# Stores and loads of y: single pairs on ScalarE's queue in place of batches on SyncE's

## What is computed

```python
def dynamic_depthwise(x, w1, b1, w2, b2):      # layers 0, 2 and 3
    pooled = x.mean(axis=(2, 3))
    hdn = relu(pooled @ w1 + b1)
    kernels = (hdn @ w2 + b2).reshape(b, 32, 3, 3)   # one 3x3 kernel per sample and channel
    return depthwise_conv(x, kernels, pad=1)

def sign_conv(x, W):                           # layer 1
    return conv(sign(x), sign(W), pad=1)       # 32 channels to 32
```

## Time and profile before

| | |
|---|---|
| median of 3 runs | 4350.15 us (4338.25 to 4359.49) |
| the profiled execution, its own time | 4354.15 us |
| its span, first to last instruction | 4352.3 us |
| granted TensorE clock, mean | 0.873 of full speed |
| busy, TensorE matmuls | 3142.5 us (72%) |
| busy, VectorE | 2069.2 us (48%) |
| busy, ScalarE | 1786.4 us (41%) |
| busy, GpSimd | 1957.0 us (45%) |
| moved by DMA | 829.46 MB, mean 191 GB/s |
| queue q1 (SyncE) | 734.28 MB, 66.5% of 16 engines' span |
| queue q10 (ScalarE) | 76.68 MB, 8.2% |
| issue to landing, median | load of a batch 26.1 us, store 23.6 us, early channel 6.4 us |

### The profile page before, as it was taken

One profiled execution on the slowest core, in us unless ns is written; L12 is line 12 of the kernel. 1 busy time (PEld: TensorE's weight loads), 2 busy tenths in 40 slices (PEclk: granted clock), 3 DMA queues, 4 the chain that ended last, 5 costly groups with the idle time before them and its releaser, 6 DMA issues.

```text
span 4352.3 us, 69714 instructions
## 1 busy us (share of the span) xinstructions
PE 3142.5 (72%) x26176; PEld 2008.6 (46%) x26176; DVE 2069.2 (48%) x6038; ACT 1786.4 (41%) x2626; POOL 1957.0 (45%) x3175
## 2 busy tenths in 40 slices
PE   0675987758876588865887667867778759777598
PEld 0443645435454354633545434554445535445355
DVE  2626643266432764327543275333844257432573
ACT  2433633335333463434534354333543436324232
POOL 1326544264432653336533464425643265431754
PEclk9987998879988798987998879888889889888799
DMA  6288697876969769596694967969678697786946
GB/s 210 57 147 168 151 318 200 155 164 140 340 175 170 159 159 322 159 195 153 182 330 119 212 148 197 306 118 216 149 217 292 109 212 165 234 270 111 200 76 218
DMA packets 589270, 829.46 MB, mean 191 GB/s; under 512 B 489731, under 2 KB 490502, under 8 KB 572550
## 3 DMA queue, kind: packets, MB, share of 16 engines
q1 hardware_dynamic: 323200, 734.28, 66.5%
q10 hardware_dynamic: 216582, 76.68, 8.2%
q0 software_dynamic: 49152, 14.05, 2.0%
HBM read 375.89 MB, written 267.45 MB: 148 GB/s over the span
## 4 chain that ended last, share of the span: by engine, by line
PE 46%; DMA 21%; DVE 9%; SPq 8%; ACT 5%; POOL 4%; ACTq 3%; issue 3%; DVEq 0%; POOLq 0%
PE acc L961 26%; PE acc L978 14%; SPq L327 6%; DMA dense_out<-arena 5%; DMA out<-y 4%; DMA arena<-x 4%; POOL y L510 4%; PE acc L1040 3%; DMA arena<-signs 3%; DVE dense_stats L860 2%; DMA signs<-arena 2%; DMA arena<-y 2%; ACT arena L599 2%; ACTq L535 2%; ACTq L606 2%
## 5 line engine op out<-in xcount | busy, mean ns | idle before, releaser
L961 PE MATMUL acc<-y,arena 64*128 64x384 f32 x9216 | 1749.3, 508 | 190.1 <-ACT y L568 129.0
L961 PEld LDWEIGHTS acc<-y,arena 64*128 64x128 f32 x9216 | 1013.6, 197 | 777.4 <-ACT y L568 229.2
L327 POOL DMA_DIRECT2D arena<-y x1536 | 790.6, 522 | 837.3 <-PE acc L978 736.4
L568 ACT ACTIVATE y<-acc 128x768 f32<-128x768 f32 x832 | 645.1, 807 | 1177.5 <-PE acc L978 1176.6
L978 PE MATMUL acc<-arena 64*128 64x384 f32 x4608 | 953.9, 509 | 195.2 <-issue 195.2
L489 POOL TENSOR_SCALAR arena<-arena,cst,fill 128x24 f32<-128x24 f32 (+1 forms) x1536 | 614.3, 419 | 701.8 <-issue 450.4
L510 POOL TENSOR_TENSOR y<-arena,y 128x3072 f32<-128x3072 f16 x88 | 529.8, 6043 | 734.5 <-DMA arena<-dense_out 734.3
L860 DVE BATCH_NORM_STATS2 dense_stats<-y 128x6 f32<-128x192 f32 x1536 | 408.0, 345 | 728.4 <-POOL y L510 728.2
L978 PEld LDWEIGHTS acc<-arena 64*128 64x128 f32 x4608 | 518.1, 196 | 422.3 <-issue 228.2
L1040 PE MATMUL acc<-arena,wd_side 128*32 128x384 fp8e4 (+1 forms) x10752 | 470.4, 329 | 290.3 <-DMA arena<-signs 231.5
L802 DVE TENSOR_SCALAR_CACHE_REDUCE y<-acc 128x768 f32<-128x768 f32 x256 | 245.1, 958 | 624.3 <-PE acc L978 624.3
(11 more groups left out here) (84 smaller groups left out, 1145.6 us busy)
## 6 DMA issues: line engine op xcount, KB each, us to landing
y<-x SPq DMA_DIRECT2D x64, 2304.0 KB, 26.1
out<-y SPq DMA_DIRECT2D x64, 2304.0 KB, 23.6
arena<-y SPq DMA_DIRECT2D x768, 141.0 KB
arena<-x SPq DMA_DIRECT2D x168, 576.0 KB, 6.4
dense_out<-arena ACTq DMA_DIRECT2D x384, 192.0 KB, 6.9
arena<-dense_out SPq DMA_DIRECT2D x192, 384.0 KB, 6.8
arena<-y SPq DMA_DIRECT2D x768, 71.9 KB
arena<-signs SPq DMA_DIRECT2D x192, 250.0 KB, 10.4
```

The lines of the kernel that those rows point to most:

```text
L327: eng.dma_start(halo[at:at + n, slot, :, d0:d0 + size], y[source:source + (n - 1) * step + 1:step, first + odd:first + odd + 3:2, s0:s0 + ...
L568: nc.scalar.activation(y[:, 2 * g:2 * g + 2, k * KN:(k + 1) * KN], acc[:, 2 * k:2 * k + 2, 0:KN], ACT.Identity, accum_out=sums[:, g, k:k + ...
L961: nc.tensor.matmul(acc[:, 2 * k + odd, 0:KN], w_center[at, slot, 2 * q + odd, :], y[at, 2 * g + odd, k * KN:(k + 1) * KN], start=turn == 0 ...
```

## The change

Every pair of channels becomes a transfer of its own (1152 KB), with its own semaphores `loaded[g]` and `stored[g]`. ScalarE issues the store of pair g of layer 3 right behind its evictions of that pair, and then, from g = 5 on, waits for the store of pair g - 5 and issues the next sample's load of it. The last five loads (pairs 11 to 15) are issued in pairs 0 to 4 of the next layer 0, behind ScalarE's eviction and ahead of `pair_signs`. SyncE keeps the first loads of sample 0, halos, early channels and sign writes. VectorE in place of ScalarE reads the eight early channels (24 to 31) of layer 3, one in each of pairs 0 to 7, behind its eviction. Waits follow: GpSimd's clearing of the stage and SyncE's loads of early channels wait for VectorE's count too, the halos of layer 0 and TensorE for single pairs.

```diff
+LOAD_LAG = 5
...
     if li == 0:
-        return [c for c in range(C) if c % BATCH_CH < 2] if s == 0 else list(range(AHEAD_FIRST, C))
+        return [c for c in range(C) if c % BATCH_CH < 2] if s == 0 else list(range(AHEAD_FIRST, AHEAD_FIRST + PAIRS))
...
 def dve_channels(s, li):
-    return [c for c in range(C) if c not in act_channels(s, li)]
+    rest = [c for c in range(C) if c not in act_channels(s, li)]
+    return rest[AHEAD_FIRST:] + rest[:AHEAD_FIRST] if li == 0 and s > 0 else rest
...
+        def load(eng, s, g):
+            at = slice(2 * g, 2 * g + 2)
+            eng.dma_start(y[:, at, :].rearrange("p c n -> p (c n)"),
+                          x[s, :, at].rearrange("p c g w -> p (c g w)")).then_inc(loaded[g], 16)
+
+        def store(eng, s, g):
+
+            wait_evicted(eng, (s * ND + ND - 1) * PAIRS + g + 1)
+            at = slice(2 * g, 2 * g + 2)
+            eng.dma_start(out[s, :, at].rearrange("p c g w -> p (c g w)"),
+                          y[:, at, :].rearrange("p c n -> p (c n)")).then_inc(stored[g], 16)
+
+        def load_next(eng, s, g):
+
+            eng.wait_ge(stored[g], 16 * (s + 1))
+            load(eng, s + 1, g)
...
             if li == 0:
-                eng.wait_ge(loaded[b], 16 * (s + 1))
+                for g in range(b * BATCH_PAIRS, (b + 1) * BATCH_PAIRS):
+                    eng.wait_ge(loaded[g], 16 * (s + 1))
...
-                    if i >= AHEAD_SLOTS:
-                        sp.wait_ge(act_stat, stat_count(act_channels, s, 0) + i - AHEAD_SLOTS + 1)
+                    last = i - AHEAD_SLOTS
+                    if last >= PAIRS:
+                        sp.wait_ge(dve_stat, stat_count(dve_channels, s, ND - 1) + last - PAIRS + 1)
+                    elif last >= 0:
+                        sp.wait_ge(act_stat, stat_count(act_channels, s, 0) + last + 1)
...
-                    store(s, b)
-                    if s < B - 1:
-                        if b > 0:
-                            sp.wait_ge(stored[b - 1], 16 * (s + 1))
-                            load(s + 1, b - 1)
-                        if b == BATCHES - 1:
-                            sp.wait_ge(stored[b], 16 * (s + 1))
-                            load(s + 1, b)
...
                 pool.wait_ge(act_stat, stat_count(act_channels, s, 0))
+                if s > 0:
+                    pool.wait_ge(dve_stat, stat_count(dve_channels, s - 1, ND - 1) + AHEAD_LATE)
...
                 for g in range(PAIRS):
                     evict(d, g)
+                    if s > 0 and g < LOAD_LAG:
+                        load_next(act, s - 1, PAIRS - LOAD_LAG + g)
                     if g > 0:
                         pair_signs(s, g - 1)
...
                 for g in range(PAIRS):
                     evict(d + 2, g)
+                    store(act, s, g)
                     if s < B - 1:
-                        if g < AHEAD_LATE:
-                            ahead_stats(s, PAIRS + g)
+                        if g >= LOAD_LAG:
+                            load_next(act, s, g - LOAD_LAG)
...
                     if li == 2 and s < B - 1:
-                        if AHEAD_LATE <= g < AHEAD_LATE + AHEAD_FIRST // 2:
+                        if g < AHEAD_LATE:
+                            wait_ahead(dve, s, PAIRS + g)
+                            channel_stats(AHEAD_FIRST + PAIRS + g, ahead[:, (PAIRS + g) % AHEAD_SLOTS])
+                        elif g < AHEAD_LATE + AHEAD_FIRST // 2:
+                            dve.wait_ge(loaded[g - AHEAD_LATE], 16 * (s + 2))
                             for c in (2 * (g - AHEAD_LATE), 2 * (g - AHEAD_LATE) + 1):
-                                dve.wait_ge(loaded[c // BATCH_CH], 16 * (s + 2))
-                                channel_stats(c)
+                                channel_stats(c, y[:, c])
...
                     if li == 0:
-                        pe.wait_ge(loaded[chunk], 16 * (s + 1))
+                        pe.wait_ge(loaded[g], 16 * (s + 1))
```

More of the change, by code:

```diff
@@ L276, in conv_preact_kernel @@
         setup_done = sem("setup_done")
-        loaded = [sem(f"loaded{b}") for b in range(BATCHES)]
-        stored = [sem(f"stored{b}") for b in range(BATCHES)]
+        loaded = [sem(f"loaded{g}") for g in range(PAIRS)]
+        stored = [sem(f"stored{g}") for g in range(PAIRS)]
         ahead_in = [sem(f"ahead_in{k}") for k in range(AHEAD_SLOTS)]
@@ L335, in wait_evicted, with wait_ahead @@
                 eng.wait_ge(acc_free[k], pairs)
+        def wait_ahead(eng, s, i):
+            eng.wait_ge(ahead_in[i % AHEAD_SLOTS], 16 * (s * AHEAD // AHEAD_SLOTS + i // AHEAD_SLOTS + 1))
+        def load(eng, s, g):
[10 more added lines that the diff above has]
+            load(eng, s + 1, g)
         def wait_halo_source(eng, bt):
@@ L355, in _ @@
         def _(sp):
[L356 to L365, removed]
             def halos(bt):
@@ L409, in load_dense @@
                                      src.rearrange("(i j) c n -> j i (c n)", j=S)).then_inc(d_loaded[n % D_SLOTS], 16)
-            for b in range(BATCHES):
-                load(0, b)
+            for g in range(PAIRS):
+                load(sp, 0, g)
             sp.wait_ge(cleared, 3)
@@ L447, in _ @@
                         load_ahead(s, PAIRS + AHEAD_SLOTS + 2 * b + i)
-                    store(s, b)
-                    if s < B - 1:
-                        if b > 0:
-                            sp.wait_ge(stored[b - 1], 16 * (s + 1))
-                            load(s + 1, b - 1)
-                        if b == BATCHES - 1:
-                            sp.wait_ge(stored[b], 16 * (s + 1))
-                            load(s + 1, b)
-            for b in range(BATCHES):
-                sp.wait_ge(stored[b], 16 * B)
+            for g in range(PAIRS):
+                sp.wait_ge(stored[g], 16 * B)
         @block.gpsimd
@@ L554, in ahead_stats @@
             def ahead_stats(s, i):
-                uses = s * AHEAD // AHEAD_SLOTS + i // AHEAD_SLOTS + 1
-                act.wait_ge(ahead_in[i % AHEAD_SLOTS], 16 * uses)
+                wait_ahead(act, s, i)
                 at = ahead[:, i % AHEAD_SLOTS, :]
@@ L618, in _ @@
             for n, c in enumerate(act_channels(0, 0)):
-                act.wait_ge(loaded[c // BATCH_CH], 16)
+                act.wait_ge(loaded[c // 2], 16)
                 channel_stats(c, y[:, c, :], ahead[:, n % AHEAD_SLOTS, :])
@@ L718, in halo_weights, with channel_stats @@
                 by_column("h", spread_h, w_halo[:, slot], BATCH_PAIRS).then_inc(halo_w_ready, BATCH_PAIRS)
-            def channel_stats(c):
+            def channel_stats(c, src):
                 parts = dense_stats[:, 0, 0:THIRDS, :]
                 for k in range(THIRDS):
-                    last = nc.vector.bn_stats(parts[:, k, :], y[:, c, k * KN:(k + 1) * KN])
+                    last = nc.vector.bn_stats(parts[:, k, :], src[:, k * KN:(k + 1) * KN])
                 link(last)
@@ L890, in _ @@
             for c in dve_channels(0, 0):
-                dve.wait_ge(loaded[c // BATCH_CH], 16)
-                channel_stats(c)
+                dve.wait_ge(loaded[c // 2], 16)
+                channel_stats(c, y[:, c])
             for s in range(B):
```

## The result

The changed kernel took 4448.58 us in the median of 4 runs (4444.88 to 4467.59), the kernel before 4352.44 us beside it. The ratio is **1.0231, 95% interval 1.0203 to 1.0259**. The forecast was 4134 us with a range of 4010 to 4320, faster. It was wrong in sign.

What follows compares the result with a forecast made beforehand. Seven handovers (layer 3 to next layer 0) each lose 60.4 us, mainly to small transfers behind whole batches on SyncE's queue. Stalls of 5 + 2 + 7 + 4 + 9 + 3 = 30 us would remain, giving 4134 us, range 4010 to 4320.

Steps and rivals of the forecast that it cites:

- alternating with q10 they take 8 x (0.303 + 0.459) = 6 us in place of 16.23: Layer 3: early channels share engines packet by packet with q10 and land in 6 us; later ones leave 2 us of stalls.
- the first stall, 5.23 us at pair 4, had no store before it and stays: 5: Layer 3, pair 4: the wait for the first early channel is unchanged, 5 us per handover.
- barely: SyncE's halos: two batches of TensorE work (24 us) just cover 12 us of landing and up to 11.83 us of issue.
- The price is the same: Layer 3 statistics: waiting for an early channel on VectorE costs what it did on ScalarE; 0 us taken.
- The 12.75 us wait for sign writes goes: Layer 0: ScalarE's wait for sign writes disappears, as they no longer stand behind loads on q1.
- 9 us of stalls and 3 of clock: Per handover: 9 us of layer 0 stalls from late loads and their halos, 3 us of clock lost behind remaining stalls.
- the mechanism at pair 12: Layer 3, pair 12: TensorE's means for the next sample wait for VectorE's statistics of load 3, a 7 us stall.
- the zero for smaller packets: Single-pair transfers: smaller packets cost 0 to 19 us of DMA time a handover, mattering only where DMAs set the pace.
- the zero for ScalarE's issues in its pair: ScalarE: issues of 0.36 to 0.77 us plus evictions take 3.1 to 3.9 of a pair's 6 us; cost 0.
- estimate of about eight transfers before issue stalls: q10: beyond about eight transfers ScalarE's issues stall, in pairs 13 to 15 of layer 3, costing 4 us.
- rival C: Back-pressure: ScalarE's issues and store waits delay evictions, losing 38 us in layer 3, 17 in layer 0; 4418 us, chance 0.10.
- Rival B: The DMA engines set the pace: the handover stays at 260 us, total about 4350 us; chance 0.10.

Runs made afterwards that it cites:

- the fastest version: Changed kernel with SyncE's early channels (layer 3) and sign writes (layer 0) issued ahead of halos, early channels read by ScalarE: 4239.41 us, ratio 0.9747.
- both orders changed: Early channels (layer 3) and sign writes (layer 0) ahead of halos: changed kernel with ScalarE as reader 4239.41 us; kernel before, one queue, 4375.17 us.

## Why the prediction was wrong

**The step that failed** is "alternating with q10 they take 8 x (0.303 + 0.459) = 6 us in place of 16.23", and with it "the first stall, 5.23 us at pair 4, had no store before it and stays: 5". I priced one early channel against one packet in turn from q10, and left the first one as it was. The rows of before showed what that misses: SyncE's order had put each batch's early channels 1.8 us ahead of its store (546.68 and 548.48 us), so nothing large stood in the way of the first. On q10 the store of pair 0 goes out at 532.1 us, 17.7 us before those channels, and one more with each pair. 4.79 us without stores became 13.21 us with them; the later channel took 16.23 us before, 16.27 without stores and 20.09 with them. In place of 5 + 2 us of stalls there, the first handover has 18 + 23 (pairs 3 and 7), and the mean layer 3 is 44 us over its undisturbed 98.9.

The price was also one of the mean, where the last part decides. A transfer adds 16 to its semaphore in single steps, and the trace has their times. Of the channel issued at 549.76 us fourteen steps came within 6.3 us, about the 6 that I reckoned, and the last two after 7.9 and 13.2. Without stores all sixteen came within 4.8. For the channel issued at 591.71 us already the first step took 8.4 us, so there the whole transfer was late; that halos ahead of it on q1, slowed in turn by q10, are the reason is my reading and not shown.

**SyncE's issue.** I allowed 11.83 us per batch of halos "barely" and gave it no cost. It cost 4.4 us where the first early channels of layer 3 stand behind it: 7.51 us without stores, 11.89 with them.

**The reader.** "The price is the same" held at the old lateness (ratio 1.0014) and not at the new one: 57 of the 96 us went when ScalarE read the late channels.

**Layer 0.** "The 12.75 us wait for sign writes goes" was wrong: 24.81 us. They no longer stand behind loads on q1, but SyncE issued them behind halos that wait for two loads from the backlog of q10; the first was ready near 696 us and went out at 714. I had reckoned 9 us of stalls and 3 of clock; layer 0 stayed at 130.5 us, 29 over 101.2. Issued in time, a sign write still took 27.55 us to land, as shown above, so SyncE's order was only a part of it.

**Right:** the mechanism at pair 12. In the changed kernel the earlier stalls hid it (the pair took 6.8 us, no stall for the 7 forecast); once they were gone it showed, with 4 to 17 us in the fastest version. Right too were the zero for smaller packets (1.0014 with batches and 1.0019 with pairs on SyncE) and the zero for ScalarE's issues in its pair. The issues of stores and loads in the changed kernel (line's row: durations in ns, least, median, most) are

```profile
L353 ACTq DMA_DIRECT2D out<-y x128: 338/338/367, 532.1 to 4440.8; - x128
...
L346 ACTq DMA_DIRECT2D y<-x x112: 334/494/2692, 583.1 to 3976.3; - x112
```

The estimate of about eight transfers before issue stalls, priced at 4 us, did not hold: at 677.81 us, with eight earlier stores and loads on q10 not yet landed, a load's issue took 0.35 us.

So **rival C**, whose time of 4418 us came nearest, was the wrong reason: with five pairs no eviction waited for a store. In layer 0 the signs did, 40.5 us in 12 waits over the whole run, 6 us a handover where C had 55. **Rival B** was wrong too. The Trainium skill ("DMA: Bandwidth & Descriptors", section "Issuing engines are not separate DMA queues") says that spreading the issue saves only the issuing time. The change by itself gained nothing, which agrees, but the reason was not that the DMA engines were the bound; and with both orders changed two queues took 4239.41 us where one took 4375.17, some 19 us a handover against 5.8 of issue time in my estimate. There the measurement decides, with the reserve that the two kernels also differ in batches and pairs and in how far a load stands behind its store. While VectorE waited at pair 7 of the changed kernel, the DMA engines' mean busy share, in tenths over 40 slices from 600 to 624 us, was

```profile
DMA  9997998687575533211110000000899799889980
```

The channel landed at 611.83 us, in the twentieth slice, after several slices at one to three tenths, and then the engines stood still until TensorE had moved on. My list of ways to slow down had "SyncE's issue later" and "back-pressure", each alone; it had none in which the change took away an order that someone had written.

## What to carry to other kernels

When transfers move to a queue of their own, write down for each small urgent one what stands ahead of it *and beside it* before and after; a program order that puts it ahead of the bulk is lost with the second queue. Then move the urgent ones to the front of their own queue: the same change was 2.3% slower without that and 2.1% faster with it (2.5% with ScalarE as the reader). Test the order on the old layout too, for there it can cost (0.5% here).

## What the runs showed of the hardware

- A transfer lands with the last of its 16 steps, and the last can be far behind: 5.3 us after the fifteenth for the channel issued at 549.76 us. The tail above, with the mean share at one to three tenths, lasted over 3 us before the early channel counted as landed; a mean share over a stage does not show it. Which engines are last the trace does not tell, and it was not tried.
- Issuing a batch of halos on SyncE takes longer while bulk moves, on whichever queue, for the same 8 instructions: 7.51 us with q10 empty, 11.89 with stores on it, and before the change 11.38 right behind a store on q1 itself. ScalarE's issue of a pair's store took 0.338 us in the median all the same, its loads up to 2.69. Why is open.
- In the fastest version a handover is still some 47 us over its undisturbed 200 (1726.3 us for seven). How much of that a lighter sharing could take back was not tried.
